# A gated feed-forward kernel: gate products ahead of up products, and another split of the last tile

## What is computed

```python
xq = int4_quant(y)                       # scale from the mean of |y| of the row
gate = bitlinear(xq, w_gate, s_gate)     # 512 -> 1376, weights -1, 0 or 1
up = bitlinear(xq, w_up, s_up)           # 512 -> 1376
gate = jnp.square(jax.nn.relu(gate))
inter = int8_quant(up * gate)            # scale from the largest |value| of the row
return x + bitlinear(inter, w_down, s_down)   # 1376 -> 512
```

## Time and profile before

| | us |
|---|---|
| runs shown | 221.1, 221.6, 222.94 |
| median | 221.6 |
| the profiled execution, device time | 221.94 |
| its span in the profile | 220.1 |
| PE busy | 182.1 (83%) |
| DVE busy | 168.0 (76%) |
| ACT busy | 115.2 (52%) |
| one tile in the middle, start to start on PE | 10.26 |

### The profile page before, as it was taken

The page is one execution under the profiler, slowest core; times in us unless marked ns, Lnnn a source line. Parts: engine busy times, 40 slices in busy tenths (PEclk is TensorE's granted clock), DMA queues, the critical chain, the costliest instruction groups (busy, mean ns, idle before and its releaser), DMA issues.

```text
span 220.1 us, 3405 instructions
## 1 busy us (share of the span) xinstructions
PE 182.1 (83%) x1139; PEld 94.2 (43%) x1139; DVE 168.0 (76%) x457; ACT 115.2 (52%) x182; POOL 9.6 (4%) x27
## 2 busy tenths in 40 slices
PE   1010499699859899999999999999999999997882
PEld 1010296454324345455454545444545545443340
DVE  6999677769839687787878787878678787878671
ACT  2365976599812528273554546382827364553610
POOL 4043500000000000000000000000000000000000
PEclk9999999999999999999999999999999999999998
DMA  3999049992994929485856657584949475251613
GB/s 77 386 378 284 5 108 339 300 264 55 209 224 89 231 84 230 107 232 101 223 113 195 136 169 164 143 208 111 224 111 244 89 227 111 60 121 43 150 30 76
DMA packets 43824, 36.61 MB, mean 166 GB/s; under 512 B 30240, under 2 KB 30304, under 8 KB 43808
## 3 DMA queue, kind: packets, MB, share of 16 engines
q1 hardware_dynamic: 43488, 36.40, 63.3%
q0 software_dynamic: 256, 0.00, 0.1%
q10 hardware_dynamic: 64, 0.00, 0.0%
HBM read 25.27 MB, written 4.28 MB: 134 GB/s over the span
## 4 chain that ended last, share of the span: by engine, by line
PE 54%; DVE 3%; issue 3%; DMA 2%; ACT 1%; DVEq 0%
PE down_ps L600 14%; PE gate_ps L562 13%; PE up_ps L564 12%; PE conv_ps L475 12%; PE tr_act_ps L465 2%; DMA it_int<-inter_q 2%; PE tr_dve_ps L488 1%; PE conv_ps L519 1%; DVE inter L1034 1%; ACT g L693 1%; ACT g L696 1%; DVE i_t L1058 0%; DVE inter_q L1089 0%; ACT i_t L709 0%; DVE o_sb L1105 0%
## 5 line engine op out<-in xcount | busy, mean ns | idle before, releaser
L562 PE MATMUL gate_ps<-gate_t,q_t 128*128 128x416 bf16 (+2 forms) x192 | 68.6, 357 | 3.3 <-DVE q_t L974 2.1
L564 PE MATMUL up_ps<-up_t,q_t 128*128 128x416 bf16 (+2 forms) x192 | 68.5, 357 | 0.0
L693 ACT ACTIVATE g<-gate_ps,gu_scale 128x416 f32<-128x416 f32 (+2 forms) x48 | 30.3, 631 | 65.5 <-issue 50.4
L1034 DVE SCALAR_TENSOR_TENSOR inter<-up_ps,gu_scale,g 128x416 f32<-128x416 f32 (+2 forms) x48 | 33.2, 692 | 24.1 <-ACT g L696 24.1
L600 PE MATMUL down_ps<-down_t,i_t 128*128 128x512 bf16 (+1 forms) x176 | 40.7, 379 | 3.5 <-DVE down_t L955 1.9
L475 PE MATMUL conv_ps<-toep,x_t 128*64 128x512 f32 (+3 forms) x256 | 38.0, 439 | 1.6 <-ACT x_t L652 1.5
L1038 DVE TENSOR_REDUCE imax<-inter 128x1 f32<-128x416 f32 (+2 forms) x48 | 30.3, 631 | 1.7
L562 PEld LDWEIGHTS gate_ps<-gate_t,q_t 128*128 128x128 bf16 x192 | 18.7, 97 | 25.2 <-issue 7.3
L696 ACT ACTIVATE g<-g 128x416 f32<-128x416 f32 (+2 forms) x48 | 28.1, 585 | 1.5
L600 PEld LDWEIGHTS down_ps<-down_t,i_t 128*128 128x128 bf16 (+1 forms) x176 | 16.9, 98 | 23.9 <-DVE i_t L1058 4.0
L475 PEld LDWEIGHTS conv_ps<-toep,x_t 128*64 128x64 f32 x256 | 17.0, 136 | 21.2 <-issue 15.6
(11 more groups left out here) (169 smaller groups left out, 165.6 us busy)
## 6 DMA issues: line engine op xcount, KB each, us to landing
toep<-k_back SPq DMA_DIRECT2D x16, 512.0 KB, 4.9
x_in<-in_x_dram SPq DMA_DIRECT2D x32, 128.0 KB, 3.1
x_res<-in_x_dram SPq DMA_DIRECT2D x32, 128.0 KB, 4.0
out_dram<-o_sb SPq DMA_DIRECT2D x32, 128.0 KB, 2.6
raw_down<-in_L_ffn_w_down_dram SPq DMA_DIRECT2D x2, 1376.0 KB, 8.8
raw_gate<-in_L_ffn_w_gate_dram SPq DMA_DIRECT2D x1, 1536.0 KB, 7.0
raw_up<-in_L_ffn_w_up_dram SPq DMA_DIRECT2D x1, 1536.0 KB, 14.2
raw_gate<-in_L_ffn_w_gate_dram SPq DMA_DIRECT2D x1, 1024.0 KB, 9.3
```

The lines of the kernel that those rows point to most:

```text
L562: pe.matmul(gate_ps[bank][:, 0:cn], q_t[p][:, i, :], gate_t[:, i, c0:c0 + cn], start=(i == 0), stop=(i == KB - 1))
L564: mm = pe.matmul(up_ps[bank][:, 0:cn], q_t[p][:, i, :], up_t[:, i, c0:c0 + cn], start=(i == 0), stop=(i == KB - 1))
L693: nc.scalar.activation(g2[bank][:, 0:cn], gate_ps[bank][:, 0:cn], ACT.Relu, scale=gu_scale[p][:, 0:1]).then_inc(relu_done, 1)
L1034: v.scalar_tensor_tensor(out=inter[:, c0:c0 + cn], in0=up_ps[bank][:, 0:cn], scalar=gu_scale[p][:, 1:2], in1=g2[bank][:, 0:cn], op0=ALU.mu ...
```

## The change

1. In `products` a chunk's four gate matmuls come first, then its four up matmuls. The gate matmuls wait only for the relu that read the bank before; the wait for `inter_ready` moves to the first up matmul. There are two semaphores, `gate_done` (ACT's relu waits for it) and `up_done` (DVE's product waits for it).
2. On ACT `y_round` of the next tile moves behind `relu_square(2)`, from tile 1 on. On DVE `q_copy` of the next tile moves behind the quantisation, in tiles 2 to 13.
3. In tile 15 DVE takes chunk 1 before it casts `i_t` of tile 14.
4. The last tile: DVE quantises blocks 0 to 5 and ACT blocks 6 to 10; the copies after PE's transposes are swapped (DVE the first part, ACT the second); `keep_clock(8)` becomes `keep_clock(2)`; the down product is made in two halves of 256 columns, in the banks of `conv_ps` and `up_ps0`; the residual is added for each half, and the output leaves in four stores of 64 rows by 256 columns, the last of them on ACT's queue. DVE adds the residual of tile 14 after its copy for the last tile, no longer before.

```diff
@@ products (PE)
                 wait(pe, relu_done, NC * m + c - 1)
+                for i in range(KB):
+                    mm = pe.matmul(gate_ps[bank][:, 0:cn], q_t[p][:, i, :], gate_t[:, i, c0:c0 + cn],
+                                   start=(i == 0), stop=(i == KB - 1))
+                mm.then_inc(gate_done, 1)
                 wait(pe, inter_ready, NC * m + c - 1)
                 for i in range(KB):
-                    pe.matmul(gate_ps[bank][:, 0:cn], q_t[p][:, i, :], gate_t[:, i, c0:c0 + cn],
-                              start=(i == 0), stop=(i == KB - 1))
                     mm = pe.matmul(up_ps[bank][:, 0:cn], q_t[p][:, i, :], up_t[:, i, c0:c0 + cn],
                                    start=(i == 0), stop=(i == KB - 1))
-                mm.then_inc(gu_done, 1)
+                mm.then_inc(up_done, 1)
@@ turn_last (PE)
-                keep_clock(8)
+                keep_clock(2)
@@ down (PE)
+        LAST = [(conv_ps, slice(0, L // 2)), (up_ps[0], slice(L // 2, L))]
...
                 if k == T:
-                    pe.wait_ge(it_act_copied, 1)
...
+                    pe.wait_ge(it_dve_copied, T)
+                    for bank, cols in LAST:
+                        for c in range(IB):
+                            if c == IT_SPLIT:
+                                pe.wait_ge(it_act_copied, 1)
+                            r = P if c < IB - 1 else IR
+                            mm = pe.matmul(bank[:, 0:L // 2], i_t[0:r, c, :], down_t[0:r, c, cols],
+                                           start=(c == 0), stop=(c == IB - 1))
+                        mm.then_inc(down_done, 1)
+                    return
@@ body (ACT)
                 if k == T:
-                    act.wait_ge(it_turned, 1)
+                    act.wait_ge(iscale_ready, 1)
+                    act.wait_ge(it_loaded, 16 * (T - 1))
+                    cut = slice(IT_SPLIT * P, I)
+                    nc.scalar.activation(inter_q[:, cut], inter[:, cut], ACT.Copy,
+                                         scale=iscale[:]).then_inc(inter_quant, 1)
+                    act.wait_ge(it_turned, 2)
                     act.wait_ge(down_done, T - 1)
-                    nc.scalar.copy(i_t[:, 0:IT_SPLIT, :].rearrange("p c t -> p (c t)"),
-                                   tr_act_ps[:, 0:IT_SPLIT * P // 2].bitcast(I16)).then_inc(it_act_copied, 1)
+                    nb = IB - 1 - IT_SPLIT
+                    nc.scalar.copy(i_t[:, IT_SPLIT:IB - 1, :].rearrange("p c t -> p (c t)"),
+                                   tr_dve_ps[:, 0:nb * P // 2].bitcast(I16))
...
+                    act.wait_ge(out_ready, T + 1)
+                    act.dma_start(in_dram(out, T - 1, 1)[:, LAST[1][1]],
+                                  o_sb[1][half_rows(1), LAST[1][1]]).then_inc(stored[1], 16)
                 if k < T:
                     relu_square(1)
-                if k < T - 1:
-                    y_round(m + 1)
                 if k == 0:
+                    y_round(1)
                     xt_copy(2)
                 if k < T:
                     relu_square(2)
+                if 1 <= k < T - 1:
+                    y_round(m + 1)
@@ body (DVE)
+                if k == T - 1:
+                    gated(1)
                 if 1 <= k < T:
                     dve.wait_ge(it_loaded, 16 * m)
...
-                if 1 <= k < T - 1:
+                if k == 1 or k == T - 2:
                     q_copy(m + 1, 1 - p)
...
                         v.tensor_scalar(inter_q[:, 0:I], inter[:], iscale[:], None, ALU.mult).then_inc(inter_quant, 1)
+                        if 2 <= k < T - 2:
+                            q_copy(m + 1, 1 - p)
```

More of the change, by code:

```diff
@@ L365, in body @@
                     sp.dma_start_transpose(it_int[:], inter_q[:]).then_inc(it_loaded, 16)
-                if k >= 2:
+                if k == T + 1:
+                    sp.wait_ge(out_ready, T)
+                    for half in range(2):
+                        sp.dma_start(in_dram(out, T - 1, half)[:, LAST[0][1]],
+                                     o_sb[p][half_rows(half), LAST[0][1]]).then_inc(stored[p], 16)
+                    sp.wait_ge(out_ready, T + 1)
+                    sp.dma_start(in_dram(out, T - 1, 0)[:, LAST[1][1]],
+                                 o_sb[p][half_rows(0), LAST[1][1]]).then_inc(stored[p], 16)
+                elif k >= 2:
                     sp.wait_ge(out_ready, m - 1)
@@ L596, in down @@
                 for c in range(IB):
-                    if c == IT_SPLIT and k == T:
-                        pe.wait_ge(it_dve_copied, m)
                     r = P if c < IB - 1 else IR
@@ L1039, in gated, with add_out @@
                                            apply_absolute_value=True)
+                def add_out(n, bank, cols, done):
+                    q = n % 2
+                    dve.wait_ge(down_done, done)
+                    dve.wait_ge(res_loaded[q], 32 * (n // 2 + 1))
+                    wait(dve, stored[q], 32 * (n // 2))
+                    v.scalar_tensor_tensor(out=o_sb[q][:, cols], in0=bank[:, 0:cols.stop - cols.start],
+                                           scalar=oscale[q][:], in1=x_res[q][:, cols],
+                                           op0=ALU.mult, op1=ALU.add).then_inc(out_ready, 1)
                 if k is None or 1 <= k < T:
@@ L1084, in body @@
                     step(v.tensor_scalar(gam127[:], gamma[:], EPS, 1.0 / 127.0, ALU.add, ALU.mult))
-                    step(v.reciprocal(iscale[:], gam127[:]))
                     if k != T - 1:
+                        step(v.reciprocal(iscale[:], gam127[:]))
                         if k >= 1:
```

46 lines of the change are left out of this document (23 added, 23 removed).

## The result

| | before | after |
|---|---|---|
| median, us (4 runs each) | 222.03 (221.1 to 222.94) | 216.04 (215.56 to 217.07) |
| ratio | | 0.9737, 95% interval 0.9677 to 0.9796 |
| span of the profiled execution | 220.1 | 215.3 |

Faster by 2.6%, 5.99 us between the medians, where 3.4 were forecast. The profiled execution of after is the longest of its four (217.07 device time); the spans of the other three are 213.8 to 214.6.

A forecast was written before the change was run, and what follows sets the result against it. PE was taken to bound the middle tiles at 10.26 us, with gains only where PE waits: -0.13 - 1.23 - 1.08 - 0.94 = -3.38, so 218.2 us against the median 221.6; 8 in 10 range 217.3 to 219.9.

The forecast's parts named there:

- Gate before up, in the middle tiles: Middle tiles: grouped gate matmuls let relu start 0.70 earlier in chunk 0, shortening a DVE wait; PE has no gap, 0.0.
- The two moves have a cover each: Middle tiles: `y_round` done at 6.7, needed at 7.6; `q_t` ready at 9.4 of 10.26, cover 0.86 instead of 1.17.
- Tile 2: Tile 2 and before: shorter ACT and DVE work behind the transposing DMA starts tile 3 at 80.06 instead of 80.19, -0.13.
- Tile 14: Tile 14: `qt` starts at 7.02 instead of 7.64 and the copy comes earlier, so tile 15 starts at 7.94, -1.23.
- tile 15 up to the scale: Tile 15: DVE takes chunk 1 ahead of the cast, so `iscale` comes at 7.64 instead of 8.72, -1.08.
- the end: From the scale to the span's end: fewer clock-keeping matmuls, swapped copies, halves and split stores take 8.14 instead of 9.08, -0.94.
- The clock didn't fall in the tail: Rival, last tile: the clock falls to half rate; 220.6, or 223.0 if both down products pay; chance 0.05 in all.
- the loss that the prediction weighed: Tail: transposes don't count as busy for the clock, so two clock-keeping matmuls may not hold it where eight did.
- Halves didn't cost their loads: Rival, last down product: weight loads of the 256-column matmuls stop being hidden, +2.1 in all, 220.3; chance 0.06.
- Only part arrives: Rival, tiles 14, 15 and end: late copy, cast, landing, ACT blocks or store; 219.0 to 220.2, middle 219.5; chance 0.17.
- it does nothing: Rival: early relu finds ACT busy and the last tile's halves run one after the other as before; 221.3; chance 0.03.
- `q_copy` becomes what PE waits for: Rival, 12 tiles: `q_copy` behind quantisation delays PE; 0.3 a tile eats the 3.4, 0.5 gives 224.2; chance 0.03.

The follow-up runs named there:

- part 1 alone: The kernel before with only the gate matmuls put ahead of the up matmuls, with two semaphores; 222.14 us, ratio 0.9975.
- the longer DVE operation: A useless 512-column DVE operation behind the `i_t` cast, tiles 3 to 14, added to the gates-first kernel (230.64 us) and to the changed kernel (218.99 us).
- the moves alone: The kernel before with only `y_round` behind relu and square of chunk 2 and `q_copy` behind the quantisation; 221.23 us, ratio 0.9959.

## Why the prediction was wrong in size

**The step that failed** is "Gate before up, in the middle tiles", which ends in "That shortens DVE's wait of 1.26 and frees nobody who is late. 0.0", on the ground that PE leaves no gap. The reading ahead of it failed with it, that DVE's waits for ACT "are over long before PE needs what comes of them": DVE's product of chunk 0, which starts behind the wait of 1.26, is what PE waited for. PE was the one who was late: chunk 2's gate matmuls stood behind DVE's product of chunk 0, 0.17 us in each of the tiles 3 to 13, 1.89 in all. The forecast with that term in it would have been 218.2 - 1.9 = 216.3, against 216.04. So close an agreement is in part luck: the gain was 5.99 between the medians, 4.5 to 7.2 by the interval of the ratio, and the corrected sum gives 5.3; the four runs of before beside after had 222.03 and not 221.6. I saw this very wait in tile 14 (0.45) and did not look for it where the x transposes stand in front of it; a busy share of 89.90 in 90 can't show a wait that lies under a modelled end. That the wait was real is shown by moving it by one matmul, by part 1 alone and by undoing part 1 (tiles of 10.11 to 10.16, 10.10 to 10.14 and 10.27).

**"The two moves have a cover each"** was right in its numbers and wrong in its place. In tile 13 `q_t` is ready at 190.24 + 0.42 = 190.66, PE takes it at 191.54: a cover of 0.88, 0.86 forecast. But I priced the moves only by what they might cost. They also open the loop through the transposing DMA. Without them part 1 had 1.10 of the 1.89 in its profile, nothing in tile 14, and over many runs only 0.25%. That this is the loop is shown by the longer DVE operation, and that a late DMA costs its full delay there by two tiles. That late DMAs took the gain in the other eleven runs of part 1 alone is argued, not shown: these runs left no trace. Of the fourteen kept traces, six show one such tile among the tiles 3 to 13. The spread of the twelve, 219.72 to 225.09, is wider than that of before beside them, 220.72 to 224.4 in 35 runs, which fits. The clock doesn't explain it: two of the three longest runs, 223.17 and 223.08, have a mean granted clock of 1.00.

**Tile 2**: -0.13 forecast, -0.78 in the profile. From the cast of `i_t` to tile 3 it was 5.98 in before (74.21 to 80.19) and is 5.86 in after (74.63 to 80.49): -0.12, the term that was forecast. The other 0.65 is the DMA's landing, which was taken as fixed: the cast starts 3.53 after its issue, in before 4.18. It may be more than chance: the kernels with alternating matmuls had 11.55 to 11.69 in tile 2, those with the gates first 10.50 to 11.03, apart from three (11.85, 12.34, 12.37); the one with the wait moved had 13.34. Each is of one execution, and why the landing is shorter is open.

**Tile 14** (-1.23, measured -1.16), **tile 15 up to the scale** (-1.08, measured -1.17) and **the end** (-0.94, measured -0.88) held, and so did their inner steps. The tile lasts 8.01, 7.94 forecast. The down product of tile 14 starts at 5.83 (5.92), the transposes at 8.65 (8.74), the down product of the last tile 1.15 behind them (1.14); DVE's copy of 768 columns takes 0.56 (0.55), a matmul of 256 columns 0.111 (0.109), the residual 0.48 (0.49); the last two stores are issued together, 2.8 before the end (2.80). Undoing part 3 raised the median from 216.04 to 217.19, undoing the shorter `keep_clock` to 217.5; each was measured beside other runs of before, and by the ratios it is 0.6% and 0.8%. The intervals overlap that of after, so it is the profiles that size these parts: 0.89 and 1.24 from the start of tile 15 to the end.

**The rivals.** The clock didn't fall in the tail of after: 1.00 in both windows there, and the same around the transposes and the down product with eight matmuls. It can fall there. In part 1 alone with the longer DVE operation PE waited 2.33 for `q_t` ahead of tile 15, with four transposes before, and the window from then on shows 0.67 (columns as in the earlier trace rows):

```profile
210.28:215.40 5.12, 5.12 (x18) 2.22 (x19) 3.35 (x9) 2.48 (x4) 0.00 (x0) 0.67 0.50 94
```

Tile 15 and the end took 18.52 there, without the operation 17.89. The longest waits of PE in the tail of after are 0.59 and 1.01; in part 1 alone one of 1.67 at the same place left the clock at 1.00 (200.00 to 206.00). So the loss that the prediction weighed by the rule of the Trainium skill, "TensorE: Matmul & The Clock Gate", Part 4 (PE-mode transpose), didn't come here: behind eleven transposes and a wait of 0.37 the down product ran at full rate with two clock-keeping matmuls. Whether a transpose counts for the clock isn't decided by that, since a down product of 2.4 ran just before. The prediction's own case of a fallen clock, the three matmuls of 1.44, rests on their length alone: the granted clock of that stretch (25.70 to 27.20) is given as 1.00. Halves didn't cost their loads (22 matmuls in some 2.4). "Only part arrives" and "it does nothing" are refuted by the terms. "`q_copy` becomes what PE waits for" didn't happen, nor did a DVE operation of 0.66 more in each tile bring it about.

## What to carry to other kernels

A saturated engine in a busy share isn't proof that it never waits: compare the starts of neighbouring instructions with the same pair elsewhere, and look at the weight loads, wherever a wait for a semaphore stands behind an instruction whose end is modelled. When the bounding engine gets faster, look for the closed loop (here through DVE, ACT and a DMA) that is next, add its links from start to start, and keep it shorter than the tile: without slack, each late transfer stays. Moving work out of such a loop gained nothing in the middle tiles as long as PE's own tile was the longer one (10.27 with the moves alone), so try the two together before dropping either.
